# State-space preparation on one Trainium2 core: 1+exp and its logarithm go to PSUM, and the remainder pass moves forward

## What is computed

```
dt, Bm, Cm = split(u @ x_proj)
dt = softplus(dt @ dt_proj + dt_proj_b)          # log(1 + exp(.))
for every token t:
    dA = exp(dt_t * A)                           # 128 channels x 16 states
    h  = dA * h + (dt_t * u_t) * B_t
    y  = sum over states of h * C_t
y = (y + u * D) * silu(z)
```

## Time and profile before

| | |
|---|---|
| median of 3 runs | 2171.5 us (2171.23 to 2172.33) |
| the profiled execution | 2169.19 us, of which 2167.4 us are the span |
| PE busy | 1599.9 us (74%) |
| DVE busy | 1304.6 us (60%) |
| ACT busy | 1031.5 us (48%) |
| POOL busy | 1156.8 us (53%) |
| mean granted clock of TensorE | 0.875 of full speed |
| mamba stage of layer 0, of layer 1 | `y` of the first chunk at 120.29 and 1283.94 us, of the last one at 630.96 and 1794.73 us |

### The profile page before, as it was taken

The page is one execution under the profiler, slowest core; times in us unless marked ns, Lnnn a source line. Parts: engine busy times, 40 slices in busy tenths (PEclk is TensorE's granted clock), DMA queues, the critical chain, the costliest instruction groups (busy, mean ns, idle before and its releaser), DMA issues. The chain is left out here.

```text
span 2167.4 us, 26308 instructions
## 1 busy us (share of the span) xinstructions
PE 1599.9 (74%) x4872; PEld 834.2 (38%) x4873; DVE 1304.6 (60%) x2262; ACT 1031.5 (48%) x1696; POOL 1156.8 (53%) x1151
## 2 busy tenths in 40 slices
PE   4477777777777379999971367777777778289993
PEld 3122222223246146666640122222223327256662
DVE  4399999999986001111117289999999996211102
ACT  5567776776752022322321466677776772121111
POOL 2399899998851700000017189989998891400004
PEclk9799999998985689999985689999999995589995
DMA  6677777777745342111113487777777772223313
GB/s 215 149 174 170 169 171 172 168 171 167 170 93 190 90 129 75 46 44 45 47 48 105 123 187 165 170 169 171 168 170 168 168 170 70 72 73 111 110 64 95
DMA packets 104909, 283.47 MB, mean 131 GB/s; under 512 B 19789, under 2 KB 78429, under 8 KB 94013
## 3 DMA queue, kind: packets, MB, share of 16 engines
q1 hardware_dynamic: 96680, 265.34, 50.3%
q0 software_dynamic: 8192, 17.71, 2.8%
HBM read 225.80 MB, written 57.18 MB: 131 GB/s over the span
## 5 line engine op out<-in xcount | busy, mean ns | idle before, releaser
L699 POOL TENSOR_TENSOR mamba_dbu<-mamba_rep 128x462 f32<-128x462 f32 x640 | 680.3, 1087 | 45.4 <-DMA mamba_rep<-dt_rows 44.5
L558 PE MATMUL mamba_ysum<-mamba_hc,all_sel 128*128 128x462 f32 x800 | 446.7, 645 | 243.3 <-DVE mamba_hc L753 242.2
L646 ACT ACTIVATE mamba_state<-mamba_rep,all_m_acol 128x462 f32<-128x462 f32 x640 | 390.0, 640 | 267.3 <-DVE mamba_last L768 266.3
L771 DVE TENSOR_TENSOR_SCAN mamba_state<-mamba_state,mamba_carry,mamba_dbu 128x462 f32<-128x462 f32 x400 | 453.8, 1171 | 7.7 <-ACT mamba_state L646 7.7
L558 PEld LDWEIGHTS mamba_ysum<-mamba_hc,all_sel 128*128 128x128 f32 x800 | 135.4, 203 | 527.7 <-DVE mamba_hc L753 507.4
L768 DVE TENSOR_TENSOR_SCAN mamba_last<-mamba_state,mamba_last,mamba_dbu 128x462 f32<-128x462 f32 x240 | 280.0, 1166 | 35.4 <-ACT mamba_state L646 23.0
L694 POOL TENSOR_TENSOR mamba_hcp<-mamba_last,mamba_rep 128x462 f32<-128x462 f32 x240 | 266.2, 1109 | 9.4 <-DVE mamba_last L768 8.1
L1225 DVE TENSOR_TENSOR experts_h<-experts_sg,experts_up 128x512 f32<-128x512 f32 x62 | 42.6, 688 | 371.5 <-PE experts_up L1120 313.8
L753 DVE TENSOR_TENSOR mamba_hc<-mamba_state,mamba_rep 128x462 f32<-128x462 f32 x400 | 248.1, 623 | 0.0
L553 PE MATMUL mamba_ysum<-mamba_hcp,all_sel 128*128 128x462 f32 x480 | 247.4, 599 | 0.0
L290 POOL MEMSET seq_mhalf<- 96x3 f32 x2 | 0.2, 98 | 362.0 <-POOLq L1460 362.0
(11 more groups left out here) (173 smaller groups left out, 2262.6 us busy)
## 6 DMA issues: line engine op xcount, KB each, us to landing
mamba_rep<-bc_rows SPq DMA_DIRECT2D x168, 462.0 KB, 6.9
mamba_rep<-dt_rows SPq DMA_DIRECT2D x168, 462.0 KB, 7.4
dt_rows<-mamba_dd SPq DMA_DIRECT2D x168, 115.5 KB, 7.0
weights_w<-in_L_w_dram SPq DMA_DIRECT2D x16, 1024.0 KB, 9.7
mamba_xs<-seq_scratch SPq DMA_DIRECT2D x92, 116.0 KB, 9.3
experts_xs<-slot_rows SPq DMA_DIRECT2D x62, 128.0 KB
expert_rows<-experts_eo SPq DMA_DIRECT2D x62, 128.0 KB, 1.7
slot_rows<-setup_zero SPq DMA_DIRECT2D x11, 512.0 KB
```

What stands on the lines that cost most here:

```text
L558: nc.tensor.matmul(ysum[:, 0:TC], sel[:, i // NM, :], hc[:, n % HCD, :], start=False, stop=end).then_inc(hc_summed, 1)
L646: nc.scalar.activation(state[:, STATE_BANK[i], 0:TC], rep[:, par * REP_ROWS + i // NM, :], ACT.Exp, scale=m["acol"][:, i:i + 1]).then_inc( ...
L699: pool.tensor_tensor(dbu[:, i % 4, :], rep[:, first + NG + i // NM, :], rep[:, first + 2 * NG + i % NM, :], ALU.mult).then_inc(dbu_ready, 1)
L771: nc.vector.tensor_tensor_scan(bank, bank, dbu[:, i % 4, :], carry[:, i:i + 1], ALU.mult, ALU.add).then_inc(scan_done, 1)
```

## The change

`w1` and `ln` are dropped: ACT writes 1+e to `front[:, 0]` and the logarithm to `front[:, 1]`, both PSUM. `lr` is dropped too: DVE subtracts in place in `front[:, 1]`. So each of the three DVE passes now reads one PSUM and one SBUF tensor. The pass for `rr` leaves `prep`: it becomes `prep_rr` and stands behind DVE's item 14 (between the scans of items 14 and 15), and the other two stay behind the last `hc` as `prep_dt`. On ACT 1+e stands behind item 10 instead of 11, the copy of B and C behind 12 instead of 13, and the logarithm behind 13 instead of 15; it also waits for the copy of B and C, whose source bank it overwrites. POOL's product of `dd` and u stands behind item 3 instead of 2. PE's first preparation matmul waits for DVE's `dd` of the chunk before instead of ACT's logarithm.

```diff
-AT_SILU, AT_EXP, AT_ONE, AT_LN, AT_BC, AT_DT, AT_DTU = 6, 10, 11, 15, 13, 5, 2
+AT_SILU, AT_EXP, AT_ONE, AT_LN, AT_BC, AT_DT, AT_DTU, AT_RR = 6, 10, 10, 13, 12, 5, 3, 14
...
             def prep_u(k):
                 pe.wait_ge(xs_loaded, 32 * (k + 1))
-                pe.wait_ge(front_act, START + ACTS * k)
+                pe.wait_ge(front_dve, START + DVES * k)
...
-            pe.wait_ge(front_act, START + ACTS * (NCH + 2))
+            pe.wait_ge(front_dve, START + DVES * (NCH + 2))
...
             def prep_one(k):
                 act.wait_ge(front_act, START + ACTS * k + A_EXP)
-                nc.scalar.activation(w1[:, :], ex[:, :], ACT.Copy, bias=1.0).then_inc(front_act, 1)
+                nc.scalar.activation(front[:, 0, 0:TC], ex[:, :], ACT.Copy, bias=1.0).then_inc(front_act, 1)
 
             def prep_ln(k):
-                nc.scalar.activation(ln[:, :], ex[:, :], ACT.Ln, bias=1.0).then_inc(front_act, 1)
+                act.wait_ge(front_act, START + ACTS * k + A_BC)
+                nc.scalar.activation(front[:, 1, 0:TC], ex[:, :], ACT.Ln, bias=1.0).then_inc(front_act, 1)
...
-            def prep(k):
-
+            def prep_rr(k):
+                dve.wait_ge(front_act, START + ACTS * k + A_ONE)
+                nc.vector.scalar_tensor_tensor(out=rr[:, :], in0=front[:, 0, 0:TC], scalar=1.0, in1=ex[:, :],
+                                               op0=ALU.subtract, op1=ALU.subtract).then_inc(front_dve, 1)
+
+            def prep_dt(k):
                 done = START + DVES * k
-                dve.wait_ge(front_act, START + ACTS * k + A_ONE)
-                nc.vector.scalar_tensor_tensor(out=rr[:, :], in0=w1[:, :], scalar=1.0, in1=ex[:, :],
-                                               op0=ALU.subtract, op1=ALU.subtract).then_inc(front_dve, 1)
                 dve.wait_ge(front_act, START + ACTS * k + A_LN)
                 dve.wait_ge(front_dve, done + D_R)
-                nc.vector.tensor_tensor(lr[:, :], ln[:, :], rr[:, :], ALU.subtract).then_inc(front_dve, 1)
+                nc.vector.tensor_tensor(front[:, 1, 0:TC], front[:, 1, 0:TC], rr[:, :], ALU.subtract).then_inc(front_dve, 1)
...
-                nc.vector.tensor_tensor(dd[:, 0, :], lr[:, :], rx[:, :], ALU.add).then_inc(front_dve, 1)
+                nc.vector.tensor_tensor(dd[:, 0, :], front[:, 1, 0:TC], rx[:, :], ALU.add).then_inc(front_dve, 1)
...
                         if i - 1 in ON_DVE:
                             read_out(i - 1)
+                        if i == AT_RR:
+                            prep_rr(k + 2)
                     read_out(ITEMS - 1)
-                    prep(k + 2)
+                    prep_dt(k + 2)
```

More of the change, by code:

```diff
@@ L397, in phase_mamba @@
         u, sz = sb("u", [P, UBUFS, TC]), sb("sz", [P, UBUFS, TC])
-        ab, ex, w1, ln, rx = sb("ab", [P, TC]), sb("ex", [P, TC]), sb("w1", [P, TC]), sb("ln", [P, TC]), sb("rx", [P, TC])
-        rr, lr = sb("rr", [P, TC]), sb("lr", [P, TC])
+        ab, ex, rx, rr = sb("ab", [P, TC]), sb("ex", [P, TC]), sb("rx", [P, TC]), sb("rr", [P, TC])
         dd = sb("dd", [P, 2, TC])
@@ L731, in prep @@
                 dve.wait_ge(front_dve, done + D_LR)
-                nc.vector.tensor_tensor(dd[:, 0, :], lr[:, :], rx[:, :], ALU.add).then_inc(front_dve, 1)
+                nc.vector.tensor_tensor(dd[:, 0, :], front[:, 1, 0:TC], rx[:, :], ALU.add).then_inc(front_dve, 1)
             for k in range(2):
-                prep(k)
+                prep_rr(k)
+                prep_dt(k)
             with dve.Fori(0, B) as b:
```

## The result

| | before | changed |
|---|---|---|
| median | 2171.4 us (4 runs, 2168.6 to 2172.3) | 2317.0 us (4 runs, 2309.6 to 2318.1) |
| the profiled execution | 2169.2 us | 2317.2 us, span 2315.4 |
| TensorE's mean granted clock | 0.875 | 0.832 |

The ratio is 1.0666, with a 95% interval of 1.0642 to 1.0690: 146 us slower. The forecast had 2278 us and a range up to 2304. The direction and the mechanism were as forecast; the time lies outside the range, where rival D (2320 us) had been put.

The account below looks back on a forecast made before the run. The prediction took DVE as full (519.8 of 532 us), with PE's sums setting a floor for y. Its terms, 55 + 22 - 5 + 2 + 32 = +106 us, gave 2278 us against the runs' median, range 2224 to 2304.

Parts of the forecast that it names:

- rival D: All three tail matmuls slow in most chunks and decay 11 late: 2.2 + 0.3 us a chunk, about 2320 us; chance 0.08.
- TensorE's clock: Longer PE idle stretch lets the clock fall in the three sums before y: 0.8 us a chunk, +32 us.
- decay of item 11: On ACT, 1+e ahead of item 11's decay moves it back 0.64 us, using up its slack: +2 us.
- Stall ahead of scan 14: Logarithm and two table loads before item 14's decay on ACT stall DVE 1.38 us a chunk: +55 us.
- rr between the scans: On DVE, rr between two scans adds 0.55 us a chunk, not covered by the stall: +22 us.
- PE's floor: At the chunk's end PE's sums hold y at 3.67 us after hc 14, so moving rr gains only 5 us.
- Edits at nothing: PE's wait for dd, POOL's moved product, SP's store and reload, and the prologue: covered by idle time, no cost.
- A: Rival: the clock's fall doesn't meet the tail or is short: +74 us, 2246 us; chance 0.25.
- B: Rival: no table load back ahead of item 14's decay, a stall of 0.09 us: +23 us, 2194 us; chance 0.08.
- C: Rival: only DVE's bound counts, rr falls from 1.25 to 0.55 us: -28 us, 2143 us; chance 0.05.
- E: Rival: no change, stall half as long, clock free, an unseen gain; within 4 us of 2171.5 us; chance 0.04.

Follow-up runs that it names:

- a1: The changed kernel with the logarithm put back behind item 15; 2189.7 us, 1.0090 of before.
- c2: c1 with PE taking item 13's sum ahead of item 14's; 2138.2 us, 0.9852 of before.
- c1: The changed kernel with rr back behind the last hc, 1+e behind item 11 and the logarithm behind item 15; 2167.0 us, 0.9985 of before.
- a3: The changed kernel with 1+e put back behind item 11; 2306.8 us, 1.0624 of before.
- b1: The kernel before with only the logarithm moved behind item 13 and the copy of B and C behind item 12; 2264.0 us, 1.0434 of before.
- d1: c4 with 1+e also put back behind item 11; 2260.0 us, 1.0411 of before.
- c4: The changed kernel with rr back behind the last hc, the logarithm staying behind item 13; 2289.0 us, 1.0548 of before.
- a2_fill: The changed kernel with two more zero-weight fp32 matmuls on PE between the sums of items 11 and 14; 2247.9 us, 1.0357 of before.

## Why the prediction was wrong in size

The mechanism held, and the sum failed at the size of one term: for TensorE's clock it took 32 us, and the runs show 61. That alone moves 2278 us to 2307, past the range's end of 2304; the decay of item 11, put at 2 us, adds 10 more.

The steps in their order, for 40 chunks:

1. **Stall ahead of scan 14**: forecast 55 us (1.38 each). The rows of idle time have 1.27 each: 57.7 us of waits [the row of L773 above] less the 7 us of scan 7, which a1 and c2 have as well, make 51 us. The delay is a little more, because an instruction that doesn't wait starts before the last one has ended (by 0.08 us in a1, 443.17 after 442.62 + 0.63): from the start of `hc` to that of scan 14 it is 1.89 us (450.49 to 452.38), in a1 0.55 (442.62 to 443.17), so 1.34 each, 54 us. The logarithm took 0.56 us into PSUM in place of 0.59. Right.
2. **rr between the scans**: forecast 22 us. a1 less c1 is 22.7 us (they differ also in 1+e). Right; 0.62 us for the pass was right too.
3. **PE's floor**: forecast -5 us; c1 shows -3, with `y` at 3.67 in all of its chunks in layer 0. Right, and c2 shows that the floor was PE's.
4. **Decay of item 11**: forecast +2 us. Measured 13.3 us of waits, where the kernel before has 1.1: 12 us. Mis-sized: I priced an ordinary chunk, with 0.06 us of slack left, and counted the four chunks of the kernel before in which PE's dt matmul comes late. What the moved 1+e adds to a late chunk was about right (waits of 0.81 to 0.95 us; with 1+e back behind item 11, in a3, 0.20 to 0.30), but there are 15 of them. In 14 of these slow matmuls at the chunk's beginning still start 11.3 us and more after the last `y`, and the dt matmul comes 13.5 to 13.6 us after it, elsewhere 12.6 to 13.0; in the four chunks before it came after 13.5 to 13.9 us. The remaining one is the first chunk of layer 1.
5. **Edits at nothing**: PE's wait for `dd`, POOL's move and the PSUM writes cost nothing that shows: a1 and c1 contain them all.
6. **TensorE's clock**: the step that failed, "I take 0.8 us, a third: +32 us". Measured 109.9 - 48.5 = 61 us, 1.5 us a chunk. The bounds (0 to 90 us) held; the third was a guess at the phase between idle stretch and fall. The runs showed that this phase isn't spread evenly: in the changed kernel 39 of 40 chunks have a slow tail, and b1 and d1, with some 2.25 us idle instead of 2.79, have one in 21 and 22 of 40. It isn't the idle length alone: c4, with 2.24 us, has 31.

The sum of the measured terms is 54 + 23 - 3 + 12 + 61 = 147 us, against 146. Rival D held the case (slow tails in most chunks, and decay 11 late) with a chance of 0.08; the chances were wrong more than the list. That its 2320 us is so near is in part luck: 2.2 + 0.3 us in every chunk would be 100 us on top of A's 2246, so 2346; measured were 1.5 + 0.3. Rivals A (no clock price), B (no load back) and C (DVE alone decides) fell: by a2_fill, by the two loads in ACT's rows, and by c1. E (no change) fell by the result.

Of the two rules of the Trainium skill ("ScalarE: Activation LUTs") that the prediction weighed: the drain of 1380 ns on top of a table load doesn't show in the changed kernel either (448.53 + 1.28, next activation at 449.83), and a load stands between logarithm and decay (450.40), so the rule by which one set serves both doesn't hold for this program.

What stays open is what decides between two chunks with the same idle time. The experiments show that idle time ahead of the tail is needed, and that 1.24 and 1.43 us bring no slow tail in any of 40 chunks; but with 2.27 us about half of the chunks escape, and with 2.79 us still one in the changed kernel and four in a3.

## What to carry to other kernels

Before a table switch is moved, look at which instruction stands right behind it and how long ago its buffer came free: the same 3.2 us cost nothing behind the last item; behind item 13 they cost 54 us directly and 61 more through PE's clock, together with the 0.55 us of rr, which lengthen the same idle stretch. When a pass is made cheaper, ask what ends next: here PE's sums ended together with DVE's passes, so halving one pass gave 3 us, reordering the sums 2 us, and both together 32 us. A short stall of one engine can have PE run the work behind it at the lower level; if that work is what all wait for, give the full slow rate a good chance: here it was 1.5 of at most 2.2 us a chunk, and a third of the bound was too little.

## What the runs showed of the hardware that was not expected

Idle stretches of 2.2 to 2.8 us between fp32 matmuls were enough for TensorE's lower level to show in the matmuls right behind them (1.54 us from start to start in place of 0.78), in 21 of 40 chunks at 2.27 us and in 39 of 40 at 2.79. Two matmuls of no use in the stretch made the whole kernel 69 us faster. The lengths repeat: with a slow tail a chunk of the changed kernel is mostly 30.4 or 31.1 us long, the longer ones being those with a late decay of item 11, and without slow tails (a2_fill) it is 28.7.
